# A gated cross-attention block on one core: the scaled rows of x are copied within SBUF into a float32r tile and transposed from there

## What is computed

```python
q = layernorm(x) @ W.T + b
logits = q @ ctx.T + (1 - mask) * -1e9
x = x + tanh(g_xattn) * (softmax(logits) @ ctx)
x = x + tanh(g_ffn) * (layernorm(x) @ sign(weight).T)
```

## Time and profile before

| | |
|---|---|
| median of three runs | 302.42 us |
| the profiled execution, its own time | 298.64 us |
| its span, first to last instruction | 296.8 us |
| granted TensorE clock, mean of the span | 0.995 of 2.4 GHz |
| PE busy | 285.9 us, 96% of the span |
| ACT busy | 255.4 us, 86% |
| DVE busy | 250.3 us, 84% |
| POOL busy | 214.5 us, 72% |
| DMA queue of SP | 44.19 MB, 45.8% of 16 engines |

### The profile page before, as it was taken

One profiled execution on the slowest core, in us unless ns is written; L12 is line 12 of the kernel. 1 busy time (PEld: TensorE's weight loads), 2 busy tenths in 40 slices (PEclk: granted clock), 3 DMA queues, 4 the chain that ended last, 5 costly groups with the idle time before them and its releaser, 6 DMA issues.

```text
span 296.8 us, 9236 instructions
## 1 busy us (share of the span) xinstructions
PE 285.9 (96%) x2329; PEld 276.0 (93%) x2329; DVE 250.3 (84%) x783; ACT 255.4 (86%) x740; POOL 214.5 (72%) x585
## 2 busy tenths in 40 slices
PE   7799999999999999999999999999999999999982
PEld 6689999999999999999999999999999999999972
DVE  4568988988898898889889888988988898898883
ACT  2599999999999999999999999999999999999841
POOL 3566777787777777877777787777778777777543
PEclk9999999999999999999999999999999999999998
DMA  4933445644444554444455444445544544441112
GB/s 133 329 99 98 135 142 185 184 154 151 145 159 136 184 184 152 145 168 137 143 174 184 153 144 164 149 145 164 184 160 143 175 141 143 158 151 71 73 54 90
DMA packets 33538, 44.39 MB, mean 150 GB/s; under 512 B 3504, under 2 KB 17136, under 8 KB 33520
## 3 DMA queue, kind: packets, MB, share of 16 engines
q1 hardware_dynamic: 33520, 44.19, 45.8%
HBM read 27.40 MB, written 16.78 MB: 149 GB/s over the span
## 4 chain that ended last, share of the span: by engine, by line
PE 90%; DMA 2%; SPq 2%; POOL 1%; DVE 1%; issue 1%; ACT 1%; POOLq 0%; DVEq 0%; ACTq 0%
PE ffn_ps L655 20%; PE pv_ps L637 18%; PE l_ps L621 16%; PE ctx_ps L556 11%; PE x1t_ps L627 9%; PE xt_ps L589 9%; PE pt_ps L602 5%; PE ctx_ps L548 3%; DMA x_in<-in_x_dram 2%; POOL y L316 0%; POOL rstd L280 0%; DVE x_lo L519 0%; SPq L210 0%; DVE c L508 0%; ACT ffn_scaled L396 0%
## 5 line engine op out<-in xcount | busy, mean ns | idle before, releaser
L280 POOL TENSOR_TENSOR rstd<-ve,minus_half 128x2 f32<-128x2 f32 x128 | 89.4, 699 | 10.0
L621 PE MATMUL l_ps<-m_sb,x_t 128*128 128x77 f32 x512 | 78.7, 257 | 0.2 <-ACT x_t L377 0.2
L342 ACT ACTIVATE xs<-x_in,shift,rstd 128x256 f32<-128x256 f32 x128 | 75.7, 593 | 0.5 <-POOL shift L291 0.5
L621 PEld LDWEIGHTS l_ps<-m_sb,x_t 128*128 128x128 f32 x512 | 74.6, 191 | 0.5 <-ACT x_t L377 0.5
L627 PE MATMUL x1t_ps<-ident,x 128*128 128x128 f32 x256 | 68.8, 273 | 0.0
L637 PE MATMUL pv_ps<-ctx_v,p_t 77*128 77x256 f32 x256 | 66.1, 380 | 0.0
L655 PE MATMUL ffn_ps<-wf_t,x_hi 128*128 128x256 f32 x256 | 56.6, 303 | 2.5 <-DVE x_lo L519 2.4
L527 DVE SCALAR_TENSOR_TENSOR x<-pv_ps,c,x_in 128x256 f32<-128x256 f32 x128 | 55.3, 472 | 0.4 <-PE pv_ps L637 0.4
L316 POOL TENSOR_TENSOR y<-ffn_scaled,x 128x256 f32<-128x256 f32 x64 | 46.4, 726 | 9.2 <-ACT ffn_scaled L396 9.2
L408 ACT ACTIVATE prob<-neg_l,neg_max 128x77 f32<-128x77 f32 x128 | 44.6, 351 | 9.3 <-DVE neg_max L511 9.3
L519 DVE TENSOR_TENSOR x_lo<-x1t_ps,x_hi 128x512 fp32r<-128x512 f32 x64 | 43.9, 686 | 9.5 <-ACT x_hi L403 9.5
(11 more groups left out here) (48 smaller groups left out, 476.2 us busy)
## 6 DMA issues: line engine op xcount, KB each, us to landing
x_in<-in_x_dram SPq DMA_DIRECT2D x64, 256.0 KB, 2.7
out_dram<-y SPq DMA_DIRECT2D x64, 256.0 KB, 2.0
ctx_v<-in_ctx_dram SPq DMA_DIRECT2D x32, 154.0 KB
mask_in<-in_mask_BxSxS_ik_dram SPq DMA_DIRECT2D x32, 154.0 KB, 3.2
wq_raw<-in_L_xattn_W_dram SPq DMA_DIRECT2D x1, 256.0 KB, 3.0
wf_raw<-in_L_ffn_weight_dram SPq DMA_DIRECT2D x1, 256.0 KB, 6.4
bq_col<-in_L_xattn_b_dram SPq DMA_DIRECT2D x1, 1.0 KB, 2.8
g_raw<-in_g_xattn_dram SPq DMA_DIRECT2D x1, 0.5 KB, 3.5
```

Of the source, the lines that this page charges most:

```text
L280: pool.tensor_tensor(res[:, i], ve[:, i], minus_half[:], ALU.pow).then_inc(res_done, 1)
L342: act.activation(xs[:, n % 2, j], x_in[:, n % N, j], ACT.Identity, scale=rstd1[:, n % R, j:j + 1], bias=shift1[:, n % R, j:j + 1]).then_in ...
L621: ins = pe.matmul(l_ps[:, j * K:(j + 1) * K], x_t[:, r % 2, c, j * P:(j + 1) * P], m_sb[:, c, r % R], start=(c == 0), stop=(c == C - 1))
```

## The change

For batches 4 to 59, SP copies the scaled rows of the batch, `xs[:, i]`, to a second tile `xs_r` of type float32r, with a transfer from SBUF to SBUF of 256 KB. The bytes are unchanged: the destination is addressed as float32, so nothing is rounded. PE transposes these batches from `xs_r`, with an identity `ident_r` that is also float32r and that DVE makes at the start. Batches 0 to 3 and 60 to 63 are transposed from `xs` in float32 as before. PE waits for the transfer (`xs_moved`, one semaphore for each of the two buffers) instead of for `xs_done`; SP waits for `xs_done`. The new transfer is the first in SP's slot.

```diff
+        ident_r = sb("ident_r", [P, P], F32R)
+        xs_r = sb("xs_r", [P, 2, T, D], F32R)
...
+        def moves(t0, n):
+            return not isinstance(t0, int) or MOVE_FIRST <= t0 + n < MOVE_END
+        def moved(t0, n):
+            return t0 * (DMA // 2) + DMA * ((n - MOVE_FIRST) // 2 + 1)
...
+        MOVE_FIRST = 4
+        MOVE_END = NB - 4
...
+            def move_xs(t0, n):
+                i = n % 2
+                sp.wait_ge(xs_done, T * (t0 + n + 1))
+                sp.dma_start(xs_r[:, i].bitcast(F32), xs[:, i]).then_inc(xs_moved[i], DMA)
             def slot(t0, r):
                 t = t0 + r
+                if moves(t0, r + 1):
+                    move_xs(t0, r + 1)
                 if exists(t0, r + AHEAD):
                     at_least(sp, x1_done, t - 2)
                     load_x(t0, r + AHEAD)
...
             stats1(0)
+            dve.wait_ge(ident_ready, 2)
+            dve.tensor_copy(ident_r[:], ident[:]).then_inc(ident_r_ready, 1)
...
             def transpose_x(t0, n):
-                pe.wait_ge(xs_done, T * (t0 + n + 1))
+                if moves(t0, n):
+                    pe.wait_ge(xs_moved[n % 2], moved(t0, n))
+                else:
+                    pe.wait_ge(xs_done, T * (t0 + n + 1))
                 at_least(pe, xt_done, t0 + n)
                 for c in range(C):
                     for j in range(T):
-                        ins = pe.transpose(xt_ps[:, c, j * P:(j + 1) * P],
-                                           xs[:, n % 2, j, c * P:(c + 1) * P], ident[:])
+                        if moves(t0, n):
+                            ins = pe.transpose(xt_ps[:, c, j * P:(j + 1) * P].bitcast(F32R),
+                                               xs_r[:, n % 2, j, c * P:(c + 1) * P], ident_r[:])
+                        else:
+                            ins = pe.transpose(xt_ps[:, c, j * P:(j + 1) * P],
+                                               xs[:, n % 2, j, c * P:(c + 1) * P], ident[:])
                 ins.then_inc(xt_psum, 1)
```

More of the change, by code:

```diff
@@ L125, in flamingo_block @@
         half_ready = sem("half_ready")
+        ident_r_ready = sem("ident_r_ready")
         gate_ready = sem("gate_ready")
@@ L142, in flamingo_block @@
         xs_done = sem("xs_done")
+        xs_moved = [sem(f"xs_moved{i}") for i in range(2)]
         negmask_done = sem("negmask_done")
@@ L594, in _ @@
             m_step(1, 2)
+            pe.wait_ge(ident_r_ready, 1)
             def slot(t0, r):
```

## The result

The changed kernel takes 304.02 us, the median of 20 runs, against 301.21 us for 20 runs of the kernel before. The ratio is 1.0116, with a 95% interval of 1.0077 to 1.0155: about 3.5 us slower, where 4.5 us faster were forecast. The ratios here leave out executions that are over 1.5% above the fastest of the same kernel, the medians don't. The range of 293.5 to 308 held the time, because it reached up to a late move; the sign of the forecast was wrong.

What follows compares the result with a forecast made beforehand. The prediction took PE to bound the loop; shorter transposes gain 3.9 us in odd and 0.6 in even slots, the move and the rest cost nothing: 302.42 - 4.5 = 297.9 us, range 293.5 to 308.

Steps and rivals of the forecast that it cites:

- What bounds the kernel: In the loop PE never stops (180.00 of 180.00 us busy); transposes of the scaled rows are 10.2% of its chain.
- The price of a transpose: On PE, a scaled-row transpose falls from 110 ns to 75 in float32r, 0.14 us less in each slot.
- a load in transpose mode fits into 67 ns: On PE, the weight load of 128 columns keeps up with the transposes, as key transposes follow each other in 67 ns.
- The second rival: On PE, the weight load paces float32r transposes at 107 to 110 ns, so nothing is gained: 302.4 us; chance 0.18.
- What reaches the end: At PE's last product, waiting for x1_lo: 0.14 us gained in 28 odd slots, 0.02 in 28 even ones, together 4.5 us.
- a shorter slot moves them together and the 0.05 us stays: In even slots, c1, y and x1_lo shift with PE, so PE's load still comes 0.05 us after x1_lo.
- The move: At the slot's head, the transfer fits between ACT's last xs and PE's transposes: 2.62 us in even slots, 2.31 in odd.
- I take the store's 2.0: The SBUF to SBUF transfer lands after 2.0 us, like the store of the same size; the load takes 2.7.
- Nothing is ahead of it in the queue: On SP's queue, the move is issued some two microseconds after the last store, with nothing before it.
- SP's answer: SP starts the move 0.21 us after xs is finished, as it does for the store after y.
- The first rival: The move lands late and PE waits, from a landing L of 2.2 us, costing 28 x (L - 2.2); chance 0.25.
- The cover of the rest: SP's loads, some 1.5 us later for x, still arrive in time; DVE's identity copy falls into idle time; cost nothing.

Runs made afterwards that it cites:

- e2: The changed kernel without the transfer: ACT writes xs rounded to float32r and all 64 batches are transposed in float32r; ratio to before 0.9997, 48 slots 206.08 us.
- e3: The changed kernel with the halves of xs made, and the move issued, half a slot earlier; ratio to before 1.0003, 48 slots 206.13 us.
- e5: e3 without DVE's c1: ACT applies tanh(g_xattn) as a scale when copying the transposed probabilities; ratio to before 0.9959, 48 slots 203.58 us.
- e10: e2 with c1 removed and its factor applied by ACT, as in e5; ratio to before 0.9921, 48 slots 203.71 us.
- e9: The changed kernel with its transfer split into two halves of 128 KB, the first sent as soon as ACT has made it; ratio to before 0.9999, 48 slots 207.48 us.
- e1: The changed kernel with its transfer kept but the moved rows transposed in float32; ratio to before 1.0237, 48 slots 216.58 us.
- e6: The kernel before, with c1 removed and its factor applied by ACT, as in e5; ratio to before 1.0014, 48 slots 207.13 us.
- e4: The kernel before with rows of 24 transposes of several kinds on an empty PE at its start; float32r 87 ns, 85 with 64 moving columns.
- e8: The kernel before with rows of 16 float32r transposes between float32 rows at its start; float32r 88 ns, float32 108, float32r with 64 weight columns 63.

## Why the prediction was wrong

**What bounds the kernel.** Right: PE alone, and the transposes were 10% of it. e2, e3, e5 and e10 show that PE's time there counts.

**The price of a transpose.** The step that mis-sized it is "a load in transpose mode fits into 67 ns", read from float32 key transposes and taken over to float32r. The float32r load of 128 columns takes 84 to 88 ns and sets the pace. The term was 0.14 us a slot and measured 0.07 to 0.08. The second rival (107 ns, nothing gained) was as far off on the other side. The chain of the changed kernel seems to confirm the forecast with its 0.30 us for four transposes; but the matmuls behind them grew from 0.95 to 1.02 there. A group's price is read from the distance between marks outside the group.

**What reaches the end.** The place was right: `x1_lo`, and behind it `c1` and POOL's `y`. The sentence "a shorter slot moves them together and the 0.05 us stays" failed. `c1` moves with PE, POOL's `y` doesn't: it comes 4.0 us after the `y` of the odd slot, whether that slot takes PE 4.16 us (before) or 4.08 (e2, e3). So `y` and the end of `c1` came up to 0.08 us later relative to PE, and three of four even slots grew by 0.04 to 0.08 instead of shrinking by 0.02. With the landing out of the way the gain is 1.0 us in 48 slots (e3), where the forecast's terms make 24 x 0.16 = 3.8.

**The move.** This step decided the sign. "I take the store's 2.0" was 0.3 too short even where nothing is close ahead: the median landing is 2.3. "Nothing is ahead of it in the queue" was wrong for odd slots. The new wait at the head of the slot holds back the loads behind it. When the move is issued at 141.60, the mask's load and the store had been issued 2.7 and 2.1 us before, and neither had landed. Such a move lands mostly after 2.5 to 2.9 us; why some with the same transfers ahead still land after 2.3 (the one at 150.37) the runs don't show. SP's answer, 0.21 us in the prediction, was 0.03 for each of the 56 moves; that hid part of the error. In the order of SP's program the move carries its wait itself, while the store's wait is an instruction ahead of it; that this makes the difference was not tried.

The first rival named the mechanism, and its formula, 28 x (L - 2.2), was set up with an answer 0.18 too long: with SP's true answer and the true saving of 0.08 it decides from 2.33. The 25 moves for odd slots between 40 and 260 us landed after 2.65 us on average, by which the 24 odd slots of the measure would lose 24 x 0.32 = 7.7 us. The slots themselves lost less: the 24 odd ones take 4.41 us on average, 0.25 more than before, together 6.0 us. The 24 even ones take 4.44, 0.03 less, and give 0.7 back. Rounding apart, these are the 5.2 us that the 48 slots lost; why the odd slots lost less than the landings say was not worked out. Most even slots stand at 4.39 to 4.40: a stall makes PE's odd slot longer than POOL's way from `y` to `y` (4.35 us against 4.14 in one case), so `y` comes earlier relative to PE, after 1.56 us, and with it the end of `c1`.

**Luck.** That 304.02 lies in the range is owed to the rival that the forecast held for the less likely one (0.25 against 0.47): the range was drawn wide enough to take in a landing of 2.4. The forecast of 297.9, a ratio of 0.985, would have been too low even with the move in time: e3 has a ratio of 1.0003 (0.9961 to 1.0046).

**The cover of the rest.** The loads behind the move reached their users in time, as said, and DVE's copy cost nothing. That the loads' delay would come back to the move itself was not seen.

## What to carry to other kernels

A transfer that takes the place of a semaphore is paid in latency, and its cover is measured from the last writer to the first reader, per kind of slot. Two to three tenths of a microsecond decided here, and starting it half a slot earlier (e3, 6.2 us of the loop) or sending half of it early (e9, 4.8) was worth more than the faster instruction (4.3, e1 against the change, a part of it e1's lower clock). A wait put at the head of an in-order queue also moves what stands behind it, and that can come to stand ahead of the next transfer.

When the bounding engine gets faster, look for pairs of operations on other engines that meet now. Ask which of the two follows the bounding engine and which doesn't, and where they will meet then: the edit of `c1` brought nothing before the change (e6) and 2.5 us of the loop after it (e5 against e3).

## What the runs showed of the hardware beyond that

A copy of 256 KB from SBUF to SBUF took longer to land (2.3 us) than a store of the same size to HBM in the kernel before (2.0), and SP spent 0.48 us on issuing it against 0.36 for the store. The stores took longer too when the moves were there: 2.4 us in the change.

A two-column operation of DVE with two inputs took 0.52 to 0.70 us in all 32 even slots of the kernel before, where it started behind POOL's `y` and ended 0.01 to 0.02 us after it, and 0.15 to 0.17 us in the 32 odd ones, where they don't overlap.

The high clock was lost in a row of transposes. In e4 the granted clock was 1.00 up to 19.5 us, 0.50 (the lower level, 1.2 GHz) from 19.6 to 22.9 us, and 1.00 again from 23.1 us. Before it fell PE had done 24 float32r and 24 float32 transposes with 64 moving columns each (15.4 to 19.1 us) and begun a row with 64 weight columns. Stretches of PE: us, busy, clock, DMA share, GB/s:

```profile
17.50:19.00 1.50, 1.50 (x26) 1.00 0.20 57
19.20:21.30 2.10, 2.10 (x24) 0.59 0.00 1
21.40:24.70 3.30, 3.30 (x26) 0.76 0.00 0
24.80:27.00 2.20, 2.20 (x23) 1.00 0.00 0
```

PE was busy in all of these stretches. In e8, whose rows with fewer columns have 16 transposes each and stand between rows of full ones, the granted clock stayed at 1.00. Why it fell in e4 was not tried.
